# Expert stage of a four-block transformer kernel: four buffers for gathered rows and results, gathers six tiles ahead of the additions, addresses straight from the row table

## The chip, the cores and the metric

The kernel runs on one core of a Trainium2 chip. The metric is the device time of one execution in microseconds (us). Three runs of the kernel before took 780.53, 781.83 and 781.97 us, so the median is 781.83 us. Everything is computed in float32.

## The reference, cut to what matters

`x` has 16 sequences of 128 tokens with 256 features, 2048 rows in all. Four blocks are added to it one after the other, each on a normalised copy of the rows: a cross-attention, a slot block with 64 slots, a second cross-attention with 16 heads, and a mixture of 8 experts. The change touches only the last one:

```python
scores = softmax(x @ gate_w.T)                       # 2048 x 8
topk_ids, topk_w = grouped_topk(scores)              # best 2 of 4 groups, then best 2 experts; weights sum to 1
combine = zeros((T, 8)).at[arange(T)[:, None], topk_ids].add(topk_w)
gate, up = split(einsum('th,eih->tei', x, w13_weight))   # 256 -> 2 x 512 per expert
act = silu(gate) * up * combine[:, :, None]
out = einsum('tei,ehi->th', act, w2_weight)          # 512 -> 256, summed over the experts
```

A row has a weight other than zero for two experts only, so only those two are worth computing.

## The kernel before, in words

**Stages.** The first three blocks are software-pipelined over four groups of four sequences. They end at about 480 us of the span. The last normalised rows, each with its 8 expert weights behind it (`ROW` = 264 numbers), are stored in a table in device memory (`xh_d`), and the sum so far goes to `out_d`. A routing stage (up to about 503 us) sorts the 4096 pairs of row and expert by expert and cuts them into `NT` = 39 tiles of up to 128 rows, each tile for one expert. It leaves `row_no` (L189, one column of 128 row numbers per tile) and `e_id` (the expert of each tile). VectorE says that they are ready with `routed` (L1392).

**One tile of the expert stage** passes through these steps; t is the tile's number. All weights are in SBUF by then.

- `fetch(t)`, GpSimd, L364: an indirect DMA gathers the tile's 128 rows of `xh_d` into one of two buffers `XI`. Its addresses come from a column of their own, `row_in[u]`, and not from `row_no`.
- `pick(t)`, VectorE, L1396 to L1399: takes the weight of each row for this expert (`row_w`), and copies the row numbers of tile t+2 into `row_in[u]` (L1397).
- `turn_in(t)`, TensorE, 2 transposes into PSUM; `turned`, ScalarE, L586: copies them to `XIT`.
- `gate_up(t)`, TensorE, L948: 4 matmuls of 128x128 by 128x512, shown as 8 records. `gate(t)`, ScalarE, L590: Silu of the gate half. It waits for both halves (`gu_ps`). `gated(t)`, VectorE, L1404: Silu times weight times up.
- `turn_act(t)`, TensorE, 4 transposes; `turned(t)`, VectorE, L1408: copies them to `HAT`.
- `down(t)`, TensorE, L963: 4 matmuls of 128x128 by 128x256 (8 records). `answer(t)`, ScalarE, L595: copies the result to one of two buffers `YO`, which lie in `OT` (`y_ok`).
- `number(t)`, VectorE, L1412: copies the row numbers of tile t from `row_no` into `row_out[u]` (`no_ok`). It waits for `turns`, which GpSimd raises when it starts the addition before.
- `add(t)`, GpSimd, L374: an indirect DMA with addition adds the 128 results to rows of `out_d`. It waits for `y_ok`, for the landing of `add(t-1)` (`added`), and for `no_ok`.

Transposes on TensorE all have the line of a helper, L621.

**The order** on each engine is written by hand. Step t of TensorE is `turn_in(t+2)`, `gate_up(t+1)`, `down(t-1)`, `turn_act(t)`. Step t of ScalarE is `turned(t+2)`, `gate(t+1)`, `answer(t-1)`. Step t of VectorE is `pick(t+2)`, `gated(t+1)`, `turned(t)`, `number(t-1)`. These steps run in a loop of 18 turns with two steps each, with a few written out before and after it. GpSimd does `fetch(t+5)` right after `add(t)` (its constant `AHEAD` = 4 counts from the fetch that stands ahead of an addition), in a loop of 17 turns, two fetches and two additions a turn. `fetch(t)` waits until tile t-2 has been picked (L361) and transposed (L362), since it takes that tile's buffer.

```python
pool.wait_ge(picked_ok, t - 1)     # L361
pool.wait_ge(xt_ps, t - 1)         # L362
```

At the very end SyncE waits until all additions have landed (L293).

Of the kernel before, what the change touches and what calls it, by code (L numbers as in the profile page):

```python
# [7 lines left out]
ALU = mybir.AluOpType  # L8
# [3 lines left out]
P = 128  # L12
B, S, D = 16, 128, 256
# [13 lines left out]
NT = B * S * NPICK // P + NE - 1  # L27
EPS = 1e-5
# [32 lines left out]
def build(nc, x_d, ctx_d, ctxT_d, keep_d, fold_d, rows_d, experts_d, xh_d, out_d):  # L61
    with ExitStack() as stack:
# [67 lines left out]
        def split(v, t):  # L130
# [58 lines left out]
        row_no = sb("row_no", [P, NT + 2], mybir.dt.int32)  # L189
        row_w = [sb(f"row_w{u}", [P, 1]) for u in range(2)]  # L190
        row_w8 = [sb(f"row_w8{u}", [P, NE]) for u in range(2)]
        row_in, row_out = ([sb(f"{t}{u}", [P, 1], mybir.dt.int32) for u in range(2)] for t in ("row_in", "row_out"))
        at = KEEP["wih"][0]
        assert KEEP["aW2"][0] + KEEP["aW2"][1] - at >= 2 * (ROW + D + 2 * INTER)
        XI = [keep[:, at + ROW * n:at + ROW * (n + 1)] for n in range(2)]
        at += 2 * ROW
# [4 lines left out]
        YO = [spare_ot[:, D * n:D * n + D] for n in range(2)]  # L201
# [17 lines left out]
        weights_ok, weights_in, asked = sem("weights_ok"), sem("weights_in"), sem("asked")  # L219
        g_diff, g_exp, picks, counted, routed = (sem(t) for t in ("g_diff", "g_exp", "picks", "counted", "routed"))  # L220
        xi_in = [sem(f"xi_in{u}") for u in range(2)]
        xt_ps, xt, gu_ps, silu, act_ok, ha_ps, ha, y_ps, y_ok, picked_ok, no_ok, turns, added = (
            sem("e_" + t) for t in ("xt_ps", "xt", "gu_ps", "silu", "act_ok", "ha_ps", "ha", "y_ps", "y_ok", "picked_ok", "no_ok", "turns", "added"))
# [7 lines left out]
        AHEAD = 4  # L231
        XT_PS, Y_PS = ps[:, 4, 0:D], [ps[:, 5 + u, 0:D] for u in range(2)]

        def tiles_of(eng, step):
# [62 lines left out]
        def _(pool):  # L297
# [94 lines left out]
        def _(act):  # L392
# [186 lines left out]
            act.sem_inc(turns, 1)  # L579
            act.sem_inc(y_ok, 2)  # L580
# [3 lines left out]
            def turned(t, u):  # L584
                act.wait_ge(xt_ps, t + 1)
                act.copy(XIT[u], XT_PS.rearrange("p (k n) -> p k n", k=KD)).then_inc(xt, 1)  # L586

            def gate(t, u):
                act.wait_ge(gu_ps, t + 1)
                act.activation(HA[u], ps[:, 2 * u, :], ACT.Silu).then_inc(silu, 1)  # L590
# [6 lines left out]
            def step(t, u, half):  # L597
                turned(t + 2, u)
                gate(t + 1, 1 - u)
                answer(t - 1, 1 - u)  # L600

            turned(0, 0)
            turned(1, 1)
            gate(0, 0)
            turned(2, 0)
            gate(1, 1)
            tiles_of(act, step)
            gate(NT - 1, 0)
            for t in range(NT - 3, NT):
                answer(t, t % 2)  # L610
# [3 lines left out]
        def _(pe):  # L614
# [320 lines left out]
            def turn_in(t, u, half):  # L935
                pe.wait_ge(xi_in[u], 16 * (half + 1))
                if not isinstance(t, int) or t:
                    pe.wait_ge(xt, t)
                for k in range(KD):
                    ins = turn(XT_PS[:, k * P:(k + 1) * P], XI[u][:, k * P:(k + 1) * P])  # L940
                ins.then_inc(xt_ps, 1)

            def gate_up(t, u):
                at = pe.value_load(e_id[0:1, bass.ds(t, 1)], min_val=0, max_val=NE - 1) * EXP_N
                pe.wait_ge(xt, t + 1)
                for g in range(2):
                    for k in range(KD):
                        ins = pe.matmul(ps[:, 2 * u + g, :], XIT[u][:, k, :], experts[:, bass.ds(at + (2 * k + g) * INTER, INTER)],  # L948
                                        start=(k == 0), stop=(k == KD - 1))
                ins.then_inc(gu_ps, 1)  # L950

            def turn_act(t, u):
                pe.wait_ge(act_ok, t + 1)
                for k in range(INTER // P):
                    ins = turn(ps[:, 7, k * P:(k + 1) * P], HA[u][:, k * P:(k + 1) * P])
                ins.then_inc(ha_ps, 1)

            def down(t, u):
                at = pe.value_load(e_id[0:1, bass.ds(t, 1)], min_val=0, max_val=NE - 1) * EXP_N
                pe.wait_ge(y_ok, t + 1)  # L960
                pe.wait_ge(ha, t + 1)
                for k in range(INTER // P):
                    ins = pe.matmul(Y_PS[u], HAT[u][:, k, :], experts[:, bass.ds(at + 2 * KD * INTER + k * D, D)],  # L963
# [3 lines left out]
            def step(t, u, half):  # L967
                turn_in(t + 2, u, half + 1)
                gate_up(t + 1, 1 - u)
                down(t - 1, 1 - u)  # L970
                turn_act(t, u)

            turn_in(0, 0, 0)
            turn_in(1, 1, 0)
            gate_up(0, 0)
            turn_in(2, 0, 1)
            gate_up(1, 1)
            turn_act(0, 0)
            tiles_of(pe, step)
            gate_up(NT - 1, 0)  # L980
            down(NT - 3, 0)
            turn_act(NT - 2, 1)
            down(NT - 2, 1)
            turn_act(NT - 1, 0)
            down(NT - 1, 0)
# [3 lines left out]
        def _(dve):  # L989
# [390 lines left out]
            dve.memset(row_no[:, NT:NT + 2], 0)  # L1380
# [13 lines left out]
            def pick(t, u, half):  # L1394
# [117 lines left out]
```

## Time and profile before

| | |
|---|---|
| runs, median (lowest to highest) | 781.83 us (780.53 to 781.97) |
| profiled execution, span from first to last instruction | 779.1 us |
| TensorE matmuls, busy | 651.9 us, 84% of the span |
| VectorE, ScalarE, GpSimd, busy | 369.5, 221.6 and 181.0 us |
| expert stage, first gather issued to the end of the span | 504.0 to 779.1 us |
| moved by DMA | 40.27 MB, mean 52 GB/s |

The profile gives no time of its own for the profiled execution beside its span; the span is 2.7 us under the median of the runs. It lists each engine's instructions with start and duration, and for idle time what ended it. A line such as "PE ps L621 <- DMA keep<-normed,row_in" reads: TensorE, about to run line 621 with its output in `ps`, waited for the DMA from the row table (`normed`) into `keep` (where `XI` lies), addressed by `row_in`. "issue" is time in which nothing that the profile shows was waited for.

### The profile page before, as it was taken

To read this page: it belongs to the slowest core of one execution; us is meant where nothing else is said; L and a number is where in the kernel's file an instruction comes from. 1 tells how busy PE (TensorE), PEld (TensorE's weight loads), DVE (VectorE), ACT (ScalarE), POOL (GpSimd) and SP (SyncE) were. 2 spreads that over 40 slices of the span, in tenths; PEclk is the share of its full clock that TensorE was granted. 3 is DMA by queue.
4 is the path that set the end of the run, shared out by engine and by line. 5 is a ranking of instruction groups with operands and counts; after the bars stand their busy time and mean duration, and the time that the engine had idled before them with its cause. 6 is when DMAs were issued, how large, how long until landed. Compare 5 with 4: busy or idle time off the path is not lost.

```text
span 779.1 us, 10605 instructions
## 1 busy us (share of the span) xinstructions
PE 651.9 (84%) x3506; PEld 451.2 (58%) x3507; DVE 369.5 (47%) x925; ACT 221.6 (28%) x361; POOL 181.0 (23%) x151
## 2 busy tenths in 40 slices
PE   4968689998799988999978973198999989898993
PEld 3746457686477863768746752145555555555552
DVE  4443649638486384685536675622232222222221
ACT  1241254431455224454124410021221212121220
POOL 2100223002330013120022100413333333334332
PEclk9987799999999998999988995589999999999998
DMA  9900100002000011000070202012222222222222
GB/s 351 407 21 1 54 1 1 2 21 94 14 0 0 20 54 54 0 0 0 0 261 36 82 0 58 7 29 41 41 41 41 40 42 34 43 35 43 36 35 26
DMA packets 20756, 40.27 MB, mean 52 GB/s; under 512 B 3872, under 2 KB 17440, under 8 KB 19456
## 3 DMA queue, kind: packets, MB, share of 16 engines
q1 hardware_dynamic: 8736, 25.16, 8.6%
q0 software_dynamic: 7488, 10.39, 8.2%
q10 hardware_dynamic: 4512, 4.46, 1.7%
q8 instruction: 12, 0.20, 0.1%
q14 instruction: 8, 0.07, 0.0%
HBM read 30.37 MB, written 9.64 MB: 51 GB/s over the span
## 4 chain that ended last, share of the span: by engine, by line
PE 56%; issue 16%; DVE 8%; DMA 8%; ACT 5%; POOL 3%; DVEq 3%; POOLq 1%; ACTq 0%
PE ps L617 33%; PE ps L948 11%; PE ps L621 8%; DMA keep<-normed,row_in 6%; PE ps L963 4%; POOL var_xh L300 1%; ACT ring L482 1%; DVE mx L1127 1%; DMA out_x<-OT,row_out 1%; DVEq L1040 1%; ACT keep L586 1%; DVE ring L1131 1%; POOL ring L357 1%; DVE rc L1137 1%; DVE XH L1008 1%
## 5 line engine op out<-in xcount | busy, mean ns | idle before, releaser
L948 PE MATMUL ps<-experts,keep 128*128 x312 | 144.7, 607 | 8.1 <-ACT keep L586 7.8
L1404 DVE SCALAR_TENSOR_TENSOR keep<-keep,row_w,ps 128x512 f32<-128x512 f32 x39 | 29.2, 749 | 151.9 <-ACT keep L590 151.9
L948 PEld LDWEIGHTS ps<-experts,keep 128*128 128x128 f32 x312 | 56.9, 192 | 70.1 <-issue 69.7
L374 POOL DMA_INDIRECT out_x<-OT,row_out x39 | 61.8, 1584 | 147.9 <-DVE row_out L1412 86.6
L963 PE MATMUL ps<-experts,keep 128*128 x312 | 73.9, 380 | 2.0 <-DVE keep L1408 2.0
L300 POOL TENSOR_TENSOR var_xh<-var_xh,minus_half 128x4 f32<-128x4 f32 x16 | 16.9, 1059 | 250.4 <-DVE var_xh L1003 250.4
L617 PE MATMUL ps<-experts,keep 128*128 128x256 f32 (+1 forms) x184 | 70.1, 533 | 5.9 <-DVE experts L1067 2.8
L963 PEld LDWEIGHTS ps<-experts,keep 128*128 128x128 f32 x312 | 59.1, 190 | 26.2 <-issue 20.1
L617 PE MATMUL ps<-ring,V 128*32 128x128 f32 x512 | 64.3, 279 | 1.5 <-DVE OT L1139 1.5
L1127 DVE TENSOR_REDUCE mx<-ps 128x8 f32<-128x1024 f32 x32 | 39.1, 1220 | 53.8 <-PE ps L617 53.8
L617 PE MATMUL ps<-ring,keep 128*32 128x128 f32 x512 | 63.5, 273 | 0.0
L590 ACT ACTIVATE keep<-ps 128x512 f32<-128x512 f32 x39 | 23.4, 599 | 133.7 <-PE ps L948 133.7
L313 POOL TENSOR_TENSOR ring<-experts,keep 128x512 f32<-128x512 f32 x32 | 33.2, 1041 | 111.5 <-PE ps L617 111.5
L617 PEld LDWEIGHTS ps<-ring,keep 128*32 128x32 f32 x512 | 56.0, 110 | 0.0
L617 PEld LDWEIGHTS ps<-experts,keep 128*128 128x128 f32 x184 | 38.4, 215 | 27.7 <-issue 18.4
L621 PE MATMUL ps<-keep 128*128 128x128 f32 x234 | 36.6, 279 | 16.6 <-DMA keep<-normed,row_in 16.6
L488 ACT COPY ring<-ps 128x1024 f32<-128x1024 f32 x32 | 32.4, 1014 | 61.3 <-PE ps L621 60.9
L617 PEld LDWEIGHTS ps<-ring,V 128*32 128x32 f32 x512 | 45.7, 109 | 6.5 <-issue 6.4
L621 PEld LDWEIGHTS ps<-keep,ring 128*128 128x128 f32 x256 | 29.3, 146 | 26.9 <-ACT ring L482 22.7
L1137 DVE RECIPROCAL rc<-ps 128x128 f32<-128x128 f32 x32 | 30.6, 956 | 29.6 <-PE ps L617 29.6
L621 PE MATMUL ps<-keep,ring 128*128 128x128 f32 x256 | 36.4, 287 | 9.5 <-ACT ring L482 9.5
L364 POOL DMA_INDIRECT keep<-normed,row_in x39 | 38.7, 992 | 23.8 <-issue 11.0
(209 smaller groups left out, 942.9 us busy)
## 6 DMA issues: line engine op xcount, KB each, us to landing
experts<-in_experts SPq DMA_DIRECT2D x8, 1536.0 KB, 16.6
keep<-in_keep SPq DMA_DIRECT2D x1, 3075.0 KB, 19.1
ring<-in_fold SPq DMA_DIRECT2D x1, 2112.0 KB, 11.2
experts<-in_x SPq DMA_DIRECT2D x4, 512.0 KB, 3.5
experts<-in_ctxT SPq DMA_DIRECT2D x4, 512.0 KB, 4.1
out_x<-X ACTq DMA_DIRECT2D x4, 512.0 KB, 3.1
normed<-XH ACTq DMA_DIRECT2D x4, 512.0 KB, 4.0
experts<-in_ctx SPq DMA_DIRECT2D x4, 384.0 KB, 3.4
```

The costliest lines, as they stand in the source:

```text
L300: pool.tensor_tensor(var[name][:, :], var[name][:, :], minus_half[:, :], ALU.pow).then_inc(s["rs_" + name], 1)
L313: pool.tensor_tensor(KB[u % 2], KT[:, t, bb * S:(bb + 1) * S].unsqueeze(1).broadcast_to([P, HT4, S]), kept("head_mask").unsqueeze(2).broad ...
L364: pool.indirect_dma_start(out=XI[u], out_offset=None, in_=xh_d, in_offset=bass.IndirectOffsetOnAxis(ap=row_in[u][:, 0:1], axis=0)).then_in ...
L374: pool.indirect_dma_start(out=out_d, out_offset=bass.IndirectOffsetOnAxis(ap=row_out[u][:, 0:1], axis=0), in_=YO[u], in_offset=None, compu ...
L488: act.copy(PQ[u % 2], ps[:, 5:7, :].rearrange("p t (h n) -> p (t h) n", h=4)).then_inc(s["pt"], 1)
L617: ins = pe.matmul(out, w, m, start=(k == 0), stop=(k == len(pairs) - 1))
L621: return pe.transpose(out, t, ident)
L948: ins = pe.matmul(ps[:, 2 * u + g, :], XIT[u][:, k, :], experts[:, bass.ds(at + (2 * k + g) * INTER, INTER)], start=(k == 0), stop=(k == K ...
L963: ins = pe.matmul(Y_PS[u], HAT[u][:, k, :], experts[:, bass.ds(at + 2 * KD * INTER + k * D, D)], start=(k == 0), stop=(k == INTER // P - 1))
L1127: dve.tensor_reduce(mx[u % 2][:, :], sc, AXX, ALU.max)
L1137: dve.reciprocal(rc[u % 2][:, :], bank(o)[:, S:2 * S])
L1404: dve.scalar_tensor_tensor(HA[u], HA[u], row_w[u][:, 0:1], ps[:, 2 * u + 1, :], ALU.mult, ALU.mult).then_inc(act_ok, 1)
```

## The change

`XI`, `YO`, `row_w` and `row_w8` have four buffers (`DEEP` = 4) instead of two. `row_in` and `row_out` go, with the copies L1389, L1390, L1397 and L1412, the memset L1380 and the semaphores `asked`, `turns` and `no_ok`. Both indirect DMAs read their addresses from the tile's column of `row_no`. `fetch(t)` waits for tile t-4 instead of t-2, and `fetch(t+6)` comes right after `add(t)`. GpSimd's part has no loop any more, since its addresses are fixed columns. The loops of the other three engines have 8 turns of four steps, with five steps written out ahead. `gu_ps` becomes `g_ps` after the gate half and `u_ps` after the up half: Silu waits for the first alone, `gated` for both. The waits that protect buffers are written anew: `down(t)` waits for `answer(t-2)` and comes to that wait after the one for `ha`, and `answer(t)` waits until `add(t-4)` has landed. The order of the steps on TensorE, ScalarE and VectorE is as before.

```diff
+DEEP, AHEAD = 4, 6
-        row_no = sb("row_no", [P, NT + 2], mybir.dt.int32)
-        row_w = [sb(f"row_w{u}", [P, 1]) for u in range(2)]
-        row_in, row_out = ([sb(f"{t}{u}", [P, 1], mybir.dt.int32) for u in range(2)] for t in ("row_in", "row_out"))
+        row_no = sb("row_no", [P, NT], mybir.dt.int32)
+        row_w = [sb(f"row_w{u}", [P, 1]) for u in range(DEEP)]
...
-        YO = [spare_ot[:, D * n:D * n + D] for n in range(2)]
+        YO = [spare_ot[:, D * n:D * n + D] for n in range(DEEP)]
...
+        FIRST = DEEP + 1
         def tiles_of(eng, step):
-            with eng.Fori(0, (NT - 3) // 2) as m:
-                step(2 * m + 1, 1, m)
-                step(2 * m + 2, 0, m + 1)
+            for r in range(FIRST):
+                step(0, r)
+            with eng.Fori(0, (NT - 2 - FIRST) // DEEP) as m:
+                for r in range(FIRST, FIRST + DEEP):
+                    step(m, r)
...
-            def fetch(t, u):
-                if not isinstance(t, int) or t >= 2:
-                    pool.wait_ge(picked_ok, t - 1)
-                    pool.wait_ge(xt_ps, t - 1)
-                    pool.sem_inc(asked, 1)
-                pool.indirect_dma_start(out=XI[u], out_offset=None, in_=xh_d,
-                                        in_offset=bass.IndirectOffsetOnAxis(ap=row_in[u][:, 0:1], axis=0)).then_inc(xi_in[u], 16)
-            def add(t, u):
-                pool.wait_ge(y_ok, t + 3)
-                if not isinstance(t, int) or t:
-                    pool.wait_ge(added, 16 * t)
-                pool.wait_ge(no_ok, t + 1)
-                pool.sem_inc(turns, 1)
-                pool.indirect_dma_start(out=out_d, out_offset=bass.IndirectOffsetOnAxis(ap=row_out[u][:, 0:1], axis=0),
-                                        in_=YO[u], in_offset=None, compute_op=ALU.add).then_inc(added, 16)
+            def fetch(t):
+                if t >= DEEP:
+                    pool.wait_ge(xt_ps, t - DEEP + 1)
+                    pool.wait_ge(picked_ok, t - DEEP + 1)
+                pool.indirect_dma_start(out=XI[t % DEEP], out_offset=None, in_=xh_d,
+                                        in_offset=bass.IndirectOffsetOnAxis(ap=row_no[:, t:t + 1], axis=0)).then_inc(xi_in[t % DEEP], 16)
+            def add(t):
+                pool.wait_ge(y_ok, t + 1)
+                if t:
+                    pool.wait_ge(added, 16 * t)
+                pool.indirect_dma_start(out=out_d, out_offset=bass.IndirectOffsetOnAxis(ap=row_no[:, t:t + 1], axis=0),
+                                        in_=YO[t % DEEP], in_offset=None, compute_op=ALU.add).then_inc(added, 16)
...
-            for t in range(AHEAD + 1):
-                fetch(t, t % 2)
-            add(0, 0)
-            with pool.Fori(0, (NT - 1 - AHEAD) // 2) as m:
-                for t, u in ((2 * m + AHEAD + 1, 1), (2 * m + AHEAD + 2, 0)):
-                    fetch(t, u)
-                    add(t - AHEAD, u)
-            for t in range(NT - AHEAD, NT):
-                add(t, t % 2)
+            for t in range(AHEAD):
+                fetch(t)
+            for t in range(NT):
+                add(t)
+                if t + AHEAD < NT:
+                    fetch(t + AHEAD)
...
-            def answer(t, u):
-                act.wait_ge(y_ps, t + 1)
-                act.wait_ge(turns, t + 1)
-                act.copy(YO[u], Y_PS[u]).then_inc(y_ok, 1)
+            def answer(m, r):
+                act.wait_ge(y_ps, DEEP * m + r + 1)
+                if r >= DEEP:
+                    act.wait_ge(added, 16 * (DEEP * m + r - DEEP + 1))
+                act.copy(YO[r % DEEP], Y_PS[r % 2]).then_inc(y_ok, 1)
...
-                for g in range(2):
+                for g, done in enumerate((g_ps, u_ps)):
                     for k in range(KD):
                         ins = pe.matmul(...)
-                ins.then_inc(gu_ps, 1)
+                    ins.then_inc(done, 1)
...
-                pe.wait_ge(y_ok, t + 1)
                 pe.wait_ge(ha, t + 1)
+                if r >= 2:
+                    pe.wait_ge(y_ok, t - 1)
...
-            dve.tensor_copy(row_in[0][:, :], row_no[:, 0:1])
-            dve.tensor_copy(row_in[1][:, :], row_no[:, 1:2])
-            settle()
             dve.tensor_copy(mark[:, :], w_sum[:, 0:1]).then_inc(routed, 1)
...
-                dve.tensor_copy(row_in[u][:, :], row_no[:, bass.ds(t + 2, 1)])
...
-            def number(t, u):
-                dve.wait_ge(turns, t + 1)
-                dve.tensor_copy(row_out[u][:, :], row_no[:, bass.ds(t, 1)]).then_inc(no_ok, 1)
```

## Rows read from the trace of the kernel before

**Rows 1.** The page: busy us of each engine, share of the span, instructions.

```profile
PE 651.9 (84%) x3506; PEld 451.2 (58%) x3507; DVE 369.5 (47%) x925; ACT 221.6 (28%) x361; POOL 181.0 (23%) x151
```

**Rows 2.** Busy time by stretch: engines, granted clock, DMA share, GB/s.

```profile
200.00:300.00 100.00, 91.39 (x620) 68.28 (x620) 63.05 (x141) 41.12 (x60) 16.21 (x16) 1.00 0.07 25
...
560.00:580.00 20.00, 18.91 (x70) 11.46 (x69) 5.45 (x18) 4.04 (x9) 7.15 (x7) 1.00 0.24 40
```

**Rows 3.** Who waited for whom, 480 to 779 us: total us, times, longest.

```profile
PE ps L621 <- DMA keep<-normed,row_in: 16.6, 19, 5.5
...
PE ps L948 <- ACT keep L586: 7.8, 17, 0.5
```

**Rows 4.** Timeline of one pair of steps, 590 to 605 us: start, us, work.

```profile
590.67 0.82 PE L621 MATMUL ps<-keep 128*128 128x128 f32 x6
590.87 0.37 ACT L595 COPY OT<-ps 128x256 f32<-128x256 f32 x1 [1.13 <-PE ps L963]
...
591.91 0.14 DVE L1412 COPY row_out<-row_no 128x1 int32 x1
...
592.90 1.59 POOL L374 DMA_INDIRECT out_x<-OT,row_out  x1 [4.51 <-DVE row_out L1412]
...
594.79 0.99 POOL L364 DMA_INDIRECT keep<-normed,row_in  x1 [0.30 <-issue]
...
597.68 0.43 PE L621 MATMUL ps<-keep 128*128 128x128 f32 x2 [0.59 <-DMA keep<-normed,row_in]
...
598.55 3.69 PE L948 MATMUL ps<-experts,keep 128*128 x8 [0.44 <-ACT keep L586]
598.73 1.59 POOL L374 DMA_INDIRECT out_x<-OT,row_out  x1 [2.94 <-DVE row_w L1399]
...
600.62 0.99 POOL L364 DMA_INDIRECT keep<-normed,row_in  x1 [0.30 <-issue]
```

**Rows 5.** The chain that ended last, over one such pair.

```profile
594.79 2.76 DMA keep<-normed,row_in
597.55 0.13 issue
...
610.85 0.45 PE ps L621 x2
```

**Rows 6.** Timeline of the stage's start.

```profile
502.55 0.15 DVE L1389 COPY row_in<-row_no 128x1 int32<-128x1 int32 x1
...
502.84 0.15 DVE L1392 COPY mark<-ring 128x1 f32<-128x1 f32 x1
...
519.31 3.60 PE L948 MATMUL ps<-experts,keep 128*128 x8
...
525.12 3.60 PE L948 MATMUL ps<-experts,keep 128*128 x8
...
532.54 3.70 PE L948 MATMUL ps<-experts,keep 128*128 x8 [0.45 <-ACT keep L586]
```

**Rows 7.** Timeline of the stage's end.

```profile
749.84 3.60 PE L948 MATMUL ps<-experts,keep 128*128 x8
...
760.80 0.37 ACT L595 COPY OT<-ps 128x256 f32<-128x256 f32 x1 [1.13 <-PE ps L963]
...
761.99 1.55 POOL L374 DMA_INDIRECT out_x<-OT,row_out  x1 [3.11 <-DVE row_out L1412]
...
766.52 1.55 POOL L374 DMA_INDIRECT out_x<-OT,row_out  x1 [2.97 <-DVE row_out L1412]
...
770.91 1.55 POOL L374 DMA_INDIRECT out_x<-OT,row_out  x1 [2.84 <-DMA out_x<-OT,row_out]
```

**Rows 8.** DMA from 600 to 700 us: the only queue used, and issues to landing.

```profile
q0 software_dynamic: 2880, 4.00, 24.4%
...
out_x<-OT,row_out POOLq DMA_INDIRECT x16, 3.8
keep<-normed,row_in POOLq DMA_INDIRECT x15, 2.8
```

More of the change, by code:

```diff
@@ L578, in _, with turned, gate, step @@
             store(LAST)
-            act.sem_inc(turns, 1)
-            act.sem_inc(y_ok, 2)
             exp_gate(B - GB, B)
[L584 to L590, printed above, removed]
-            def answer(t, u):
-                act.wait_ge(y_ps, t + 1)
-                act.wait_ge(turns, t + 1)
-                act.copy(YO[u], Y_PS[u]).then_inc(y_ok, 1)
[L597 to L600, printed above, removed]
+            def turned(m, r):
+                act.wait_ge(xt_ps, DEEP * m + r + 1)
+                act.copy(XIT[r % 2], XT_PS.rearrange("p (k n) -> p k n", k=KD)).then_inc(xt, 1)
+            def gate(m, r):
+                act.wait_ge(g_ps, DEEP * m + r + 1)
+                act.activation(HA[r % 2], ps[:, 2 * (r % 2), :], ACT.Silu).then_inc(silu, 1)
+            def answer(m, r):
[3 more added lines that the diff above has]
+                act.copy(YO[r % DEEP], Y_PS[r % 2]).then_inc(y_ok, 1)
+            def step(m, r):
+                turned(m, r + 2)
+                gate(m, r + 1)
+                if r:
+                    answer(m, r - 1)
             turned(0, 0)
-            turned(1, 1)
+            turned(0, 1)
             gate(0, 0)
-            turned(2, 0)
-            gate(1, 1)
             tiles_of(act, step)
-            gate(NT - 1, 0)
+            gate(0, NT - 1)
             for t in range(NT - 3, NT):
-                answer(t, t % 2)
+                answer(0, t)
         @block.tensor
@@ L933, in _, with turn_in @@
             pe.wait_ge(routed, 1)
[L935 to L938, printed above, removed]
+            def turn_in(m, r):
+                pe.wait_ge(xi_in[r % DEEP], 16 * (m + r // DEEP + 1))
+                if r:
+                    pe.wait_ge(xt, DEEP * m + r)
                 for k in range(KD):
-                    ins = turn(XT_PS[:, k * P:(k + 1) * P], XI[u][:, k * P:(k + 1) * P])
+                    ins = turn(XT_PS[:, k * P:(k + 1) * P], XI[r % DEEP][:, k * P:(k + 1) * P])
@@ L964, in down, with step @@
                                     start=(k == 0), stop=(k == INTER // P - 1))
                 ins.then_inc(y_ps, 1)
[L967 to L974, printed above, removed]
+            def step(m, r):
+                turn_in(m, r + 2)
+                gate_up(m, r + 1)
+                if r:
+                    down(m, r - 1)
+                turn_act(m, r)
@@ L975, in _ @@
+            turn_in(0, 0)
+            turn_in(0, 1)
             gate_up(0, 0)
-            turn_in(2, 0, 1)
-            gate_up(1, 1)
-            turn_act(0, 0)
             tiles_of(pe, step)
[L980 to L985, printed above, removed]
+            gate_up(0, NT - 1)
+            down(0, NT - 3)
+            turn_act(0, NT - 2)
+            down(0, NT - 2)
@@ L988, in _ @@
+            turn_act(0, NT - 1)
+            down(0, NT - 1)
         @block.vector
@@ L1379, in _ @@
                               kept("expert_no").unsqueeze(1).broadcast_to([P, NT, NE]), ALU.is_equal)
-            dve.memset(row_no[:, NT:NT + 2], 0)
             dve.wait_ge(placed, 1)
@@ L1410, in number, with gated @@
-            def number(t, u):
-                dve.wait_ge(turns, t + 1)
-                dve.tensor_copy(row_out[u][:, :], row_no[:, bass.ds(t, 1)]).then_inc(no_ok, 1)
-            def step(t, u, half):
-                pick(t + 2, u, half + 1)
-                gated(t + 1, 1 - u)
-                turned(t, u)
-                number(t - 1, 1 - u)
-            pick(0, 0, 0)
-            pick(1, 1, 0)
+            def gated(m, r):
+                dve.wait_ge(silu, DEEP * m + r + 1)
+                dve.wait_ge(u_ps, DEEP * m + r + 1)
+                dve.wait_ge(picked_ok, DEEP * m + r + 1)
+                dve.scalar_tensor_tensor(HA[r % 2], HA[r % 2], row_w[r % DEEP][:, 0:1], ps[:, 2 * (r % 2) + 1, :], ALU.mult, ALU.mult).then_inc(act_ok, 1)
@@ L1422, in _, with turned, step @@
+            def turned(m, r):
+                dve.wait_ge(ha_ps, DEEP * m + r + 1)
+                dve.tensor_copy(HAT[r % 2], ps[:, 7, :].rearrange("p (k n) -> p k n", k=INTER // P)).then_inc(ha, 1)
+            def step(m, r):
+                pick(m, r + 2)
+                gated(m, r + 1)
+                turned(m, r)
+            pick(0, 0)
+            pick(0, 1)
             gated(0, 0)
-            pick(2, 0, 1)
-            gated(1, 1)
-            turned(0, 0)
             tiles_of(dve, step)
-            gated(NT - 1, 0)
@@ L1428, in _ @@
-            for t in range(NT - 3, NT):
-                if t > NT - 3:
-                    turned(t, t % 2)
-                number(t, t % 2)
+            gated(0, NT - 1)
+            turned(0, NT - 2)
+            turned(0, NT - 1)
 def packed(parts, width, arrays):
```

46 lines of the change are left out of this document (21 added, 25 removed).

## Prediction

> **What bounds the kernel now.** I read the page first, then the busy time by stretch, the list of waits, the chain of waits, and last the timeline of one pair of steps and of both ends of the stage. The page says that TensorE is the busy engine, 84% of the span [rows 1]. In the expert stage, busy time by stretch shows it at 18.9 of 20 us with the clock at its upper level, 2.4 GHz [rows 2]. That looks like an engine-bound stage, but a busy share of nine tenths hides a regular stall. The list of waits names it: 19 times TensorE waited for a gather before a transpose, and 17 times there was a second gap of 0.44 to 0.5 us before the matmuls behind it [rows 3].
>
> The chain of waits shows how regular: in every second step it leaves TensorE and goes through a gather that takes 2.76 us from issue to landing, and 0.13 us later TensorE starts. The chain is back at the same transposes at 610.85, after starting them at 597.68, so one pair of steps takes 13.17 us [rows 4, 5]. Near the end of the loop the pair takes 13.2 us as well; I counted 17 stalled steps, the first between 525.12 and 532.54.
>
> Two rows of the stage's start give the price of a step without the stall: 525.12 - 519.31 = 5.81 us. The next step has it: 532.54 - 525.12 = 7.42 us, 1.6 us more [rows 6]. So the second gap belongs to the stall. It is credited to ScalarE's copy of the tile just transposed, but `gate_up` needs the tile before that, and in steps without a stall it starts right after the two transposes. I read it as TensorE's sequencer, which had run ahead of the array and has lost that lead.
>
> Why every second step? In the timeline the result of tile t is copied out from 590.87 to 591.24. VectorE's `number` ends at 592.05, since it stands behind `turned` of the next tile, and `add(t)` starts at 592.90, 0.85 us later. The gather behind it is issued at 594.79, lands near 597.55, and is wanted when the four transposes before it end, at 597.09 (597.68 less the 0.59 us of waiting): 0.6 us too late, with the 0.13 us of waking. The stalled step is 1.5 us longer, and so the next gather, issued at 600.62 and landing about 603.4, is in time for the transposes at about 604.2 (598.55 and 5.82 less their own 0.2) [rows 4, 8]. GpSimd is not short of time: 1.59 + 0.30 + 0.99 = 2.9 us of instructions for each tile.
>
> **The change, part by part.**
>
> *Gathers one tile further ahead, in four buffers.* The gather behind `add(t)` is now for tile t+6 and is wanted one step of 5.82 us later. Its buffer was freed by tile t+2, which was transposed in step t, well before. *Addresses from the table.* The wait for `number` goes: `add(t)` can start about 0.8 us after the copy's end at 591.24 (by the 0.85 us from `number` to the addition; bounds 0.5 and 1.1), so at 592.1 and not 592.90. The gather then lands at 592.1 + 1.89 + 2.8 = 596.8, 5.7 us after its step's beginning at 591.12, and is wanted at 2 x 5.82 = 11.6 us: 5.9 us of slack where 0.6 was missing [rows 4, 8]. The new address costs the old reads: 128 numbers, one from each partition. That each number stands in a row of 39 and not alone in its tile changes nothing that I can price; the bounds are 0 and +0.5 us on each gather, which the slack hides either way. VectorE loses 2 x 0.15 us a tile, where it had room.
>
> *What is late next.* With no stall TensorE runs step after step at 5.82 us. Each other wait at that pace: `down` needs `turned` of a tile whose transposes ended 3.4 us before. Silu and `gated` have most of a step. `add` waits for the landing of the addition before: 3.8 us from issue, and 4.53 us from one addition to the next where that wait decides at the end (766.52 - 761.99), so 1.3 us of room in 5.82 [rows 7, 8]. `answer` waits for the addition four tiles before, which landed two steps earlier. So nothing takes the stall's place.
>
> *The loop itself.* 18 turns of two steps become 8 turns of four. The first step of a turn is just the one that stalls now, so a turn's own cost on TensorE (the branch, with the sequencer's lead spent) could lie hidden in the 1.57 us. From below it is 0: after the landing TensorE starts in 0.13 us, so the branch is done by then. From above it is the whole stall, 1.57 us, 8 times, 12.6 us. I take 0: between the turns the array has 0.45 + 1.7 us or more of queued work, and the start of the loop at 519.31 shows no gap at all. What it costs if that cover is gone is a rival below.
>
> *Silu after the gate half.* It starts 1.7 us earlier and nobody waits: 0 in the steady steps. At the very end `gated(38)` lies under `down(36)` and the transposes of tile 37 already, so 0 there; bounds -0.3 and 0. *Start.* Two copies and one drain go from before `routed`: 502.84 - 502.55 = 0.29 us [rows 6]. Gathers 2 and 3 now follow at once behind gather 1, and that one may land up to 0.3 us later: bounds 0 and -0.3, I take -0.3. The first tile's matmuls run at the lower clock level as before. *GpSimd without its loop*: 78 DMAs written out, with code to be loaded. Its slack of 5.9 us covers any gap that the stage shows now. *End.* The last three additions follow one another by their landings, at 761.99, 766.52 and 770.91 [rows 7]. Their waits keep one semaphore step fewer each: 0 to -0.3 us, I take -0.1.
>
> **Sum.** The step of `gate_up(2)` starts at 519.31 and that of `gate_up(37)` at 749.84, 35 steps later: 230.53 us. At 5.82 us they take 203.7 us, 26.8 less, which is also 17 stalls of 1.57 us [rows 6, 7]. With 0.3 at the start and 0.1 at the end it is 27.2 us. The span becomes 779.1 - 27.2 = 751.9 us. The median of the runs stands 2.7 us above the span, and I keep that: 781.83 - 27.2 = 754.6 us.
>
> **Rivals.**
>
> *A turn of the loop shows.* Four steps make a body twice as long. For it speaks that the stall and the turn fall together, so the trace has no turn without a stall. Against it: the 0.13 us, and that from 600 to 700 us, through seven turns, only the queue of the gathers and additions moved anything, so no code was loaded again [rows 8]. At half the upper bound, 0.8 us x 8 = 6.3 us, the time is 761; at the whole of it 767. The Trainium skill ("Runtime: NRT & Kernel Launch", Instruction fetch mechanics) says that a taken branch to code outside the two resident blocks must load it first, and that is the rule that speaks against a longer body; the rows agree that the shorter one is resident, and no row can say it of the longer. [...]
>
> *The stall stays.* It doesn't do what it says if the gather's lead is not what ends the wait, for example because gathers queue behind additions in the DMA and move late in any order. Then a step keeps its 6.6 us and the time is 781.5. Against it: each gather takes the same 2.8 us, issued 1.9 us behind an addition.
>
> *Slower: the additions become the bound.* Each waits for the one before to land. If closer spacing of the transfers, or one more gather in flight, stretches the landing from 3.8 us to beyond 5.8 (with the 0.75 us to wake GpSimd, more than 6.6 us per tile), the stage follows them. At 7.0 us of landing it is 7.75 us x 38 tiles, against 6.6 x 38 now, 44 us more: 826. Against it: the 16 DMA engines are busy 24% of the time [rows 8], an addition already follows another after 598.73 - 592.90 = 5.83 us in every second step [rows 4], and the landings don't stretch there.
>
> **How the numbers follow.** The forecast, 754.6, has a chance of 0.80; the turn of the loop shown by 2 us or more 0.12; the stall stays in full or nearly so 0.04; the additions bound it 0.04. The forecast's own uncertainty is about 2 us: half a microsecond in total of small edits, 0.02 us on a step of 5.82 times 37, and runs that spread by 1.4 us. The range reaches up into the loop's case, to 761, and down to 751.5, where a step would be 5.75 us. What this kernel's measurement can tell from no change is about 0.2%, 1.6 us. Faster by more than that: 0.80 + 0.12 and half of the stalled case, 0.94. Same: 0.02. Slower: 0.04.
>
> **What would show it.** In the profile after, the list of waits should have TensorE wait for gathers at the stage's start only (2 times or so, where there were 19), and no gap before `gate_up` behind it. Eight records of L948 should start every 5.82 us, and the chain of waits from 510 us on should be TensorE alone until the last additions. Gathers should land about 6 us before their transposes. A gap once every four steps, at the first transposes of a turn, would show the loop; additions that start 0.75 us after the landing of the one before, in the middle of the stage, would show the DMA bound. The prediction is wrong if a step is over 6 us without either, for then something that the stall covered costs time on TensorE itself.

## Result, and the profile after

| | before | after |
|---|---|---|
| runs | 781.87 us (780.53 to 781.97, 4 runs) | 753.5 us (744.58 to 756.64, 4 runs) |
| ratio | | 0.9603, 95% interval 0.955 to 0.9656 |
| the same comparison again, on another chip | 782.24 us (779.25 to 785.1, 17 runs) | 753.97 us (751.4 to 756.19, 5 runs) |
| ratio | | 0.9634, interval 0.9604 to 0.9664 |

The change makes the kernel faster. The first ratio, applied to the 781.83 us from which the forecast was made, is 750.8 us (746.6 to 754.9), the second 753.2 us (750.9 to 755.6). The forecast of 754.6 us lies inside both intervals, but the first ratio's centre lies 0.7 us below the range's lower end of 751.5. The run of 756.64 us, which is also the profiled one, counts as slow and is left out of the first ratio, so that this ratio rests on three runs. One of the three, 744.58 us, pulls it down: the mean of all four runs is 0.962 of the kernel before, which would be 752.3 us.

The page of the changed kernel, where [rows 1] showed TensorE at 84%, is from an execution with a span of 754.8 us:

```profile
PE 647.9 (86%) x3506; PEld 453.4 (60%) x3507; DVE 363.4 (48%) x844; ACT 221.8 (29%) x361; POOL 180.9 (24%) x151
```

Busy time by stretch (engines in the order of the page, then granted clock, DMA share, GB/s). Where [rows 2] had TensorE busy for 18.9 of 20 us, it has no gap left in 100:

```profile
600.00:700.00 100.00, 100.00 (x378) 62.46 (x377) 28.49 (x68) 23.48 (x52) 44.60 (x35) 1.00 0.28 46
```

Who waited for whom, 480 to 760 us, where [rows 3] had 19 waits for gathers. Two are left, both at the stage's start, and the gap before `gate_up` is gone with them:

```profile
PE ps L617 <- DMA keep<-normed,row_no: 5.7, 2, 5.1
...
PE ps L945 <- issue: 0.3, 1, 0.3
```

The chain of waits is TensorE alone, 5.82 us a step (545.95 - 540.13), for 35 steps. [Rows 5] had a gather in it at every second step.

```profile
540.13 3.44 PE ps L945 x8
543.57 1.73 PE ps L962 x8
545.29 0.66 PE ps L617 x6
545.95 3.44 PE ps L945 x8
```

A steady step, to be read against [rows 4]. The result's copy ends at 534.07, the addition starts at 534.35, and its gather is issued at 536.25:

```profile
533.70 0.37 ACT L592 COPY OT<-ps 128x256 f32<-128x256 f32 x1 [2.84 <-PE ps L962]
...
534.35 1.60 POOL L375 DMA_INDIRECT out_x<-OT,row_no  x1 [2.89 <-ACT OT L592]
...
536.25 0.99 POOL L367 DMA_INDIRECT keep<-normed,row_no  x1 [0.30 <-issue]
```

The stage's start and end, against [rows 6, 7]: the first gather, the third tile's matmuls, those of tile 37, and the last three additions.

```profile
506.70 1.19 POOL L367 DMA_INDIRECT keep<-normed,row_no  x1 [3.42 <-DVE mark L1385]
...
522.52 3.60 PE L945 MATMUL ps<-experts,keep 128*128 x8
...
726.13 3.60 PE L945 MATMUL ps<-experts,keep 128*128 x8
...
737.74 1.55 POOL L375 DMA_INDIRECT out_x<-OT,row_no  x1 [3.97 <-ACT OT L592]
...
742.19 1.55 POOL L375 DMA_INDIRECT out_x<-OT,row_no  x1 [2.90 <-DMA out_x<-OT,row_no]
...
746.61 1.55 POOL L375 DMA_INDIRECT out_x<-OT,row_no  x1 [2.87 <-DMA out_x<-OT,row_no]
```

From the first gather issued to the end of the span it is 754.8 - 506.7 = 248.1 us, and was 779.1 - 504.0 = 275.1 us: 27.0 us less. The 35 steps take 726.13 - 522.52 = 203.6 us, and took 230.5. But the first gather came 2.7 us later than before, in a part of the kernel that the change leaves as it was. So the time has two parts: the stage, where the sum came out within 0.2 us, and the blocks ahead of it, which move from execution to execution. The experiments take them in turn.

### The profile page after: what moved, and what is told of

It reads as the page before. It is cut to its first block, busy times and chain, and to the rows that moved or that the text cites. A ratio compares the mean times of both kernels' runs of the same rounds, so it can differ in the third digit from the quotient of the medians.

```text
span 754.8 us, 10099 instructions
## 1 busy us (share of the span) xinstructions
PE 647.9 (86%) x3506; PEld 453.4 (60%) x3507; DVE 363.4 (48%) x844; ACT 221.8 (29%) x361; POOL 180.9 (24%) x151
## 4 chain that ended last, share of the span: by engine, by line
PE 70%; issue 10%; DVE 8%; ACT 4%; POOL 2%; DVEq 2%; DMA 2%; POOLq 0%; ACTq 0%
PE ps L613 34%; PE ps L945 18%; PE ps L617 9%; PE ps L962 8%; POOL var_xh L304 1%; ACT ring L480 1%; DVE mx L1124 1%; DMA out_x<-OT,row_no 1%; DVEq L1037 1%; DVE ring L1128 1%; POOL ring L361 1%; DVE rc L1134 1%; DVE XH L1005 1%; DVE experts L1036 1%; ACT experts L404 1%
## 5 line engine op out<-in xcount | busy, mean ns | idle before, releaser
L375 POOL DMA_INDIRECT out_x<-OT,row_no x39 | 61.7, 1583 | 129.5 <-ACT OT L592 123.7
L613 PEld LDWEIGHTS ps<-experts,keep 128*128 128x128 f32 x184 | 38.0, 213 | 26.8 <-issue 18.7
L1402 DVE COPY keep<-ps 128x512 f32<-128x512 f32 x39 | 27.0, 693 | 52.8 <-PE ps L617 52.8
L592 ACT COPY OT<-ps 128x256 f32<-128x256 f32 x39 | 14.5, 373 | 113.6 <-PE ps L962 113.6
L617 PEld LDWEIGHTS ps<-keep,ring 128*128 128x128 f32 x256 | 28.6, 143 | 26.9 <-ACT ring L480 22.7
L367 POOL DMA_INDIRECT keep<-normed,row_no x39 | 38.6, 991 | 15.0 <-issue 11.3
```

Of the source, the lines that this page charges most:

```text
L367: pool.indirect_dma_start(out=XI[t % DEEP], out_offset=None, in_=xh_d, in_offset=bass.IndirectOffsetOnAxis(ap=row_no[:, t:t + 1], axis=0)) ...
L613: ins = pe.matmul(out, w, m, start=(k == 0), stop=(k == len(pairs) - 1))
L617: return pe.transpose(out, t, ident)
L1402: dve.tensor_copy(HAT[r % 2], ps[:, 7, :].rearrange("p (k n) -> p k n", k=INTER // P)).then_inc(ha, 1)
```

## Experiments on the stage

**The changed kernel again.** No edit.

> The changed kernel once more, unaltered, beside the kernel before. My theory: the expert stage is worth 27.1 us in every execution (17 stalls of 1.57 us and 0.3 us at the start), and what went beyond that in the first comparison came from the stages ahead of it, where TensorE's clock was granted at its lower level for 7 us at a time at up to four places, each worth 3 us, in some executions and not in others. Then from the first gather to the end the profile shows 248 us as in the first profile, whatever the whole time is, and whole times lie in steps of about 3 us between 742 and 757. Rival: the expert stage itself has a faster state (744.58 us was seen once), for example without the cold first tile; then a fast execution shows less than 246 us from the first gather to the end.

It gave 753.97 us, and its profile 754.4 - 506.1 = 248.3 us from the first gather to the end. That is the first profile's 248.1 within 0.2, though the whole times spread over 751.4 to 756.2. The kernel before spread over 779.25 to 785.1 in 17 runs of the same comparison, four times as wide as the 1.4 us that I had taken from three. None of the five was near 744.58, and the steps of 3 us that I expected between whole times can't be seen in them (751.4, 753.7, 754.0, 754.2 and 756.2). The rival, a faster state of the stage itself, can't be excluded for that one run; every profile of the changed kernel and of the versions with its lead and without extra matmuls ahead of the stage has 248.1 to 249.0 us.

**Straight addresses alone.** Gathers one tile less ahead.

```diff
-DEEP, AHEAD = 4, 6
+DEEP, AHEAD = 4, 5
```

> One size: AHEAD 5 instead of 6, so the gather behind the addition of tile t is for tile t+5, as in the kernel before; addresses stay straight from the row table. In the profile of the changed kernel an addition starts 0.41 us after the step's first transposes, its gather is issued 1.9 us later and lands 2.8 us after that, 5.1 us into a step of 5.82. So my theory expects 0.7 us of slack, no stall, and the time of the changed kernel within 1 us: the straight address alone removes the stall. Rival: the lead of one more tile is what removes it, and with five tiles every second step stalls again, 13.2 us a pair, about 780 us.

It gave 759.44 us, ratio 0.9722 (0.969 to 0.9753): neither the 754 of my theory nor the 780 of the rival. From the first gather to the end it is 252.8 us, so the straight address brings 22 of the stage's 27 us. The whole time is 5.5 us above the changed kernel's, and those need the sixth tile of lead. The list of waits gives no hint of them. It reads as in the changed kernel: one wait of 5.3 us for a gather, and no regular one. The distance between steps does:

```profile
604.91 3.63 PE L945 MATMUL ps<-experts,keep 128*128 x8
...
607.07 0.99 POOL L367 DMA_INDIRECT keep<-normed,row_no  x1 [0.30 <-issue]
...
610.10 0.82 PE L617 MATMUL ps<-keep 128*128 128x128 f32 x6
...
610.89 3.69 PE L945 MATMUL ps<-experts,keep 128*128 x8
```

The gather issued at 607.07 lands about 2.8 us later, at 609.9. Its transposes are the last two of the six that start at 610.10, so they are due at 610.54: 0.7 us of slack, as expected. Yet the step takes 610.89 - 604.91 = 5.98 us and not 5.82. In a full stall `gate_up` follows 0.87 us after the two transposes start (598.55 - 597.68 in [rows 4]), and without one after 0.2; here it follows 0.35 us after them (610.89 - 610.54). I read it so: a gather that lands 0.7 us ahead of its transposes leaves too little for those 0.87 us. That the sequencer does in them what comes between the two waits (reading `e_id`, the weights' addresses) is part of this reading; no run took it apart. Steps here are 5.91 and 5.88 to 6.17 us in turn, 5.95 on average, and 0.13 us x 35 = 4.6 us is most of the 5.5.

**Neither lead nor straight address.** The copy `number`, its tile and semaphores are back, the addition reads its addresses from that copy again, and AHEAD is 5.

```diff
+            def number(m, r):
+                if r:
+                    dve.wait_ge(turns, DEEP * m + r)
...
+                dve.tensor_copy(row_out[r % 2][:, :], src).then_inc(no_ok, 1)
...
+                pool.wait_ge(no_ok, t + 1)
+                pool.sem_inc(turns, 1)
```

> The changed kernel with two things as before: VectorE's copy of the row numbers for the addition (row_out, with its two semaphores), and AHEAD 5. Four buffers, loops of four steps and the early Silu stay. My theory: the addition starts about 0.85 us after VectorE's copy, so near 1.8 us into the step, the gather lands 6.5 us into a step of 5.82, and every second step stalls by 1.5 us again: 27 us slower than the changed kernel, within 2 us of the kernel before. Rival: the two buffers were what held the gathers back, and with four of them the time stays at that of the changed kernel.

It gave 784.87 us, ratio 1.0036 (1.0017 to 1.0054). The stalls are back, 19 waits for gathers as in [rows 3], with four buffers in place. So the number of buffers by itself does nothing, and the rival falls. The gathers' own addresses stayed straight here; no run put the copy `row_in` back.

```profile
605.03 3.69 PE L949 MATMUL ps<-experts,keep 128*128 x8
...
611.41 0.43 PE L621 MATMUL ps<-keep 128*128 128x128 f32 x2 [0.52 <-DMA keep<-normed,row_no]
```

**Lead alone.** The same with AHEAD 6.

> The changed kernel with VectorE's copy of the row numbers for the addition as before, and the gathers six tiles ahead kept. So the lead alone, without the straight address of the addition. With five tiles of lead the straight address alone still cost 5.5 us over the changed kernel, since a gather that lands only 0.7 to 0.9 us before its transposes leaves TensorE's sequencer no lead. My theory: six tiles of lead and a gather issued 0.9 to 1.3 us later still leave over 4 us, so no step stalls: the time of the changed kernel within 1.5 us. Rival: the copies and the extra semaphores cost by themselves (the version with five tiles and the copies was 2.7 us slower than the kernel before), and the time is 757 us or more.

It gave 755.91 us, ratio 0.9618 (0.9585 to 0.9651), the changed kernel's within the interval, and every steady step of its profile is 5.81 or 5.82 us. The copy and its semaphores cost nothing in the steps once the gathers have lead. From the first gather to the end it is 249.0 us, 0.8 more than in the changed kernel, all of it in the last additions. By the ratios, since the third was run on another chip, the four combinations are 1.0036 (neither), 0.9722 (address), 0.9618 (lead) and 0.9634 (both): the lead alone does all of it within the intervals, the address alone most of it, and they don't add up.

**Less lead than before.** AHEAD 4.

> One size: AHEAD 4. The gather for tile t+4 then follows the addition of tile t and is wanted at the first transposes of the very step in which that addition starts. My theory of a latency loop: from a step's start 5.95 us to the result's copy, 0.28 to the addition, 1.9 to the gather's issue, 2.8 to its landing and 0.13 to the transposes, so 11.1 us a step, some 36 steps at 5.2 us more, 185 to 195 us slower than the changed kernel: about 940 us. Rival (the stall is a fixed cost of a wait, not of the lead): one stall of 1.6 us in each step, about 810 us.

It gave 1026.7 us. The direction and the mechanism are those of my theory: TensorE waited 37 times for a gather, 186.2 us in all. But I expected 11.1 us a step, and it is 13.7:

```profile
619.12 1.59 POOL L375 DMA_INDIRECT out_x<-OT,row_no  x1 [10.77 <-ACT OT L592]
621.01 0.99 POOL L367 DMA_INDIRECT keep<-normed,row_no  x1 [0.30 <-issue]
623.94 0.68 PE L617 MATMUL ps<-keep 128*128 128x128 f32 x2 [5.14 <-DMA keep<-normed,row_no]
624.85 5.46 PE L945 MATMUL ps<-experts,keep 128*128 x8 [0.23 <-issue]
...
632.79 1.59 POOL L375 DMA_INDIRECT out_x<-OT,row_no  x1 [10.79 <-ACT OT L592]
```

The eight records of `gate_up` take 5.46 us and not 3.60, since the clock falls to its lower level in every step. Over 100 us it is granted at 0.76 on average:

```profile
600.00:700.00 100.00, 62.21 (x168) 33.25 (x167) 13.14 (x29) 10.02 (x22) 18.05 (x14) 0.76 0.11 19
```

So a wait of 5.1 us a step costs 7.9 us: the wait, 1.9 us of `gate_up` at the lower clock (5.46 - 3.60), and 0.7 us between the transposes and `gate_up` (624.85 - 623.94 = 0.91 where it is 0.2), which my 11.1 had left out as well. The 1.5 us stalls of the kernel before never did that ([rows 2] have 1.00).

**Silu after both halves**, as before the change.

```diff
-                act.wait_ge(g_ps, DEEP * m + r + 1)
+                act.wait_ge(u_ps, DEEP * m + r + 1)
```

> The changed kernel, but Silu waits for the up half as before. My theory: nobody waits for Silu in any step, and at the end the last VectorE product lies under other work, so 0 us, within 0.5. Rival: the early Silu is what let the whole stage run without a gap and its loss costs 0.6 us or more a step, 20 us.

It gave 755.74 us, ratio 0.9627 (0.9598 to 0.9655), steps of 5.82 us and 248.3 us from the first gather to the end: 0, as forecast.

## Experiments ahead of the stage

The granted clock by stretch, first of the changed kernel and then of the version with extra matmuls in the earlier loop, which is told below. In [rows 2] the clock of the stretch from 200 to 300 us was 1.00; the changed kernel's execution has a fall near 200 us that the one of before did not have:

```profile
198.00:210.00 12.00, 8.91 (x23) 3.91 (x21) 4.47 (x7) 5.82 (x8) 3.83 (x3) 0.72 0.00 0
...
395.00:425.00 30.00, 22.92 (x118) 14.28 (x117) 13.46 (x20) 10.82 (x13) 7.19 (x7) 0.83 0.49 188
```

```profile
198.00:210.00 12.00, 10.27 (x47) 6.65 (x46) 4.83 (x6) 4.86 (x6) 2.41 (x2) 1.00 0.00 0
395.00:425.00 30.00, 25.66 (x179) 16.99 (x177) 15.10 (x15) 13.84 (x16) 5.16 (x5) 0.89 0.34 124
```

**Extra matmuls in the earlier loop**, 128x128 by 128x256, whose result nobody reads, in TensorE's waits of 0.7 and 0.9 us:

```diff
+                busy(1, 0, 256)
                 turn_x4(n)
+                busy(2, 0, 256)
                 turn_x3(n + 1)
```

> The changed kernel with three extra matmuls of 128x128 by 128x256 in each turn of the loop of the earlier blocks, into TensorE's waits before the transposes of the last and of the next rows; nobody reads the result. The clock falls to its lower level for 7 us some 12 us behind that place in each of three turns and once more after the loop, and each fall costs 3 us. My theory: it is the thinner work there that lets it fall, and the run of 744.58 us was one without three of the four falls; with the extra work up to three falls go, 3 to 9 us faster. Rival: three short matmuls are too little or in the wrong place, the falls stay, and the time is that of the changed kernel within 1.5 us.

It gave 749.91 us, ratio 0.9568 (0.954 to 0.9597), 5 us less than the changed kernel by the ratios (0.9568 to 0.9634). Its six runs lie in two groups: 748.56 to 748.93 with a mean clock of 0.939 to 0.941, and 750.89 to 753.29 with 0.928 to 0.933. In the profiled one the first gather came at 498.8, 7.3 us earlier than in the changed kernel's second profile, with the fall near 200 us gone and less of them after 395 us, as the two rows above show. Not all of that belongs to the extra matmuls, as the table at the end of this section shows.

**The same edit in the kernel before.**

> The kernel before, unchanged in its expert stage, with the three extra matmuls in each turn of the earlier loop. My theory: the falls of the clock belong to the earlier blocks, which the change does not touch, so they go here as well, 3 to 7 us faster than the kernel before, and the expert stage still takes 275 us. Rival: the falls came more often in the changed kernel because of it, and the kernel before gains less than 1 us.

It gave 777.47 us, ratio 0.9935 (0.9907 to 0.9963), so 5.1 us faster, as much as in the changed kernel. From the first gather to the end it still took 777.1 - 501.9 = 275.2 us. The gain is no matter of the change. But my theory had the falls go, and in this profile three are left, between 200 and 210, 305 and 310, and 410 and 415 us.

**Extra matmuls ahead of the stage**, seventeen of 128x128 by 128x512 in TensorE's waits from the last gate logits on:

```diff
+            busy(3, 6, 512)
             pe.wait_ge(picks, 2)
...
+            busy(5, 6, 512)
+            pe.wait_ge(tiles_hot, 1)
+            busy(3, 6, 512)
...
+                if k == B:
+                    busy(2, 6, 512)
...
+            busy(4, 6, 512)
             pe.wait_ge(routed, 1)
```

> The changed kernel with 17 extra matmuls of 128x128 by 128x512 whose result nobody reads, in TensorE's waits between the last gate logits and the first transposes of the expert stage. In the profile TensorE runs at its lower clock level there for 48 us, to the end of the first tile's matmuls, which take 6.4 us and not 3.4. My theory: the level is held down by TensorE's idle time, so with work in the waits the first tile's matmuls take 3.4 to 3.6 us and some transposes and the placing matmuls are shorter too: 3 to 4 us faster. Rival: the clock stays at its lower level through the extra work, which then takes twice its time and delays the stage: 1 to 4 us slower.

It gave 752.26 us, ratio 0.9587 (0.9563 to 0.9611), 3.5 us less than the 755.7 and 755.9 us of the versions without such matmuls in the same comparison; the intervals of the ratios overlap a little. From the first gather to the end it is 246.6 us, 1.6 less than 248.2. The first tile's matmuls take 4.88 us where they took 6.40, and not the 3.4 to 3.6 that I expected; the clock had risen and fell once more at their start (0.50 from 508 to 510 us, 1.00 from 498 to 506). The placing matmuls take 0.75 us for 16 and not 1.20.

```profile
500.80 0.75 PE L934 MATMUL ps<-ring 128*128 128x78 bf16 x16
...
508.88 4.88 PE L956 MATMUL ps<-experts,keep 128*128 x8 [0.28 <-issue]
```

**Both sets.**

> The changed kernel with both sets of extra matmuls: three in each turn of the earlier loop (which alone gave 749.9 us, where the changed kernel in the same comparison's unit would be near 756) and seventeen ahead of the expert stage (alone 752.3 us). My theory: they act on separate stretches of low clock and add up, 6 us and 3.5 us: about 746 us. Rival: they overlap, since the falls are counted from the same start and move when the stage ahead is shorter, and the time stays near 750.

It gave 750.58 us, ratio 0.96 (0.9563 to 0.9636), from 748.56 to 755.58: by the medians they don't add up, and my 746 was wrong. The profiled run, 748.56 us, still had the falls near 197 and 303 us.

**Two more pairs in the loop**, before the transposes of the context and before the queries, where TensorE waits 1.35 and 1.25 us:

```diff
+                busy(2, 2, 256)
                 turn_context(n + 1)
+                busy(2, 1, 256)
                 query(n + 1)
```

> As the version with both sets, and two more pairs of extra matmuls of 128x128 by 128x256 in each turn of the earlier loop, before the transposes of the context and before the queries, where TensorE waits 1.35 and 1.25 us. In the version with the loop's three, two falls of 7 us were left, near 301 and 407 us, just at this place. My theory: they go too, in most executions, and the time is 3 to 6 us less than with both sets, about 742 us. Rival: they delay the chain by what they take beyond the waits, 0.4 us or more a turn, and the falls stay: 1 to 3 us slower than with both sets.

It gave 746.53 us (744.7 to 750.14), ratio 0.9534 (0.9499 to 0.957), 4.1 us less than with both sets, as expected, if not the 742. This is the fastest version, faster than both kernels: 4.7% less than the kernel before, and 1.0% less than the changed one by the ratios (0.9534 to 0.9634). In its profile the clock stays up in two of the places where it used to fall, and nearly so in the third:

```profile
190.00:220.00 30.00, 26.95 (x139) 17.67 (x139) 17.72 (x40) 13.34 (x23) 10.25 (x10) 1.00 0.19 63
300.00:315.00 15.00, 13.27 (x63) 7.91 (x62) 8.70 (x14) 8.00 (x11) 6.43 (x5) 1.00 0.10 34
395.00:425.00 30.00, 24.83 (x182) 16.75 (x181) 16.24 (x18) 13.79 (x16) 6.14 (x6) 0.94 0.43 163
```

**The parts of each profile.** In each of the loop's three turns ScalarE takes up the queries at one place of its own, and that row can be found in every profile. In the version with two more pairs:

```profile
107.24 1.45 ACT L404 ACTIVATE experts<-ps,q_col,keep 128x512 f32<-128x512 f32 x2 [1.49 <-PE ps L613]
208.95 1.45 ACT L404 ACTIVATE experts<-ps,q_col,keep 128x512 f32<-128x512 f32 x2 [1.49 <-PE ps L613]
310.67 1.45 ACT L404 ACTIVATE experts<-ps,q_col,keep 128x512 f32<-128x512 f32 x2 [1.49 <-PE ps L613]
```

With the first gather these rows cut the span into five parts (us):

| profile | to turn 1 | turn 1 to 2 | turn 2 to 3 | turn 3 to first gather | to the end |
|---|---|---|---|---|---|
| before | 103.0 | 101.7 | 104.7 | 194.5 | 275.1 |
| changed | 104.0 | 104.4 | 104.8 | 193.5 | 248.1 |
| changed, again | 103.5 | 104.4 | 104.8 | 193.5 | 248.3 |
| AHEAD 4 | 101.8 | 101.7 | 104.7 | 194.1 | 521.7 |
| changed, extra in the loop | 101.6 | 101.7 | 104.7 | 190.8 | 248.3 |
| before, extra in the loop | 104.1 | 104.4 | 103.1 | 190.4 | 275.2 |
| changed, extra ahead of the stage | 101.3 | 104.4 | 104.8 | 193.1 | 246.6 |
| changed, both sets | 101.1 | 104.4 | 104.8 | 189.7 | 246.8 |
| changed, both and two more pairs | 107.2 | 101.7 | 101.7 | 190.3 | 247.1 |

The loop's three matmuls take 3 us off the fourth part in every profile that has them, in both kernels: 189.7 to 190.8 us, where the nine profiles without them have 193.1 to 195.1. The missing fall near 200 us is not shown to be their work, since two of the nine lack it too (101.7). Both turns at 101.7 us stand only in the last version, in one profile. By their parts the two sets do add up: 3.8 us less in the fourth part and 1.5 less in the fifth than in the changed kernel's second profile. The medians don't show it, because the first part, which comes before most of the extra matmuls, varies by 6 us, 101.1 to 107.2 over all profiles, and by 5.5 us (101.1 to 106.6) over those that have no extra matmuls in it. There too the clock falls in one execution and not in the other. The same eight matmuls with both sets, and with two more pairs:

```profile
17.80 3.68 PE L613 MATMUL ps<-experts,qk 128*128 128x512 f32 x8
```

```profile
18.89 6.63 PE L613 MATMUL ps<-experts,qk 128*128 128x512 f32 x8
```

Against the changed kernel the extra matmuls and the clock that they hold up are worth 7.4 us by the medians (753.97 - 746.53, on two chips), and no list of waits shows them.

## Why the prediction was right, and where it was not

*The steps.* Right: 5.82 us each, 203.7 us forecast for 35 and 203.6 measured. The stalls were 26.8 us and are gone. The whole change was to gain 27.2 us. The stage gained 27.0 from its first gather on, and 27.3 with the 0.3 us ahead of that gather.

*The cause of the stall.* Right, and narrower than I put it. The two edits that I named, the lead and the straight address, are each nearly enough. For the second I had the addition start 0.8 us after the result's copy; it starts 0.28 us after it (534.35 - 534.07), and the 0.85 us after `number` belonged to the longer chain of semaphores. With the true figure the slack is 6.5 us and not 5.9, of no effect here.

*The loop's turns.* I took 0 of a possible 12.6 us. All steps are 5.81 or 5.82 us, turns included, so 0 was right. By the Trainium skill ("Runtime: NRT & Kernel Launch", Instruction fetch mechanics) a body beyond the two resident blocks would be loaded again at each turn; the body of four steps shows no gap at its turns, and from 600 to 700 us of the changed kernel, again, no queue but that of the gathers and additions moved anything.

*What is late next.* Nothing, as forecast. The additions' landings stay at 3.8 us and the gathers' at 2.8 with closer spacing.

*Start and end.* The two copies' 0.3 us at the start came: VectorE's last instruction before the first gather follows the row table by 0.27 us and no longer by 0.56. But from the first gather to the third tile's matmuls it is now 522.52 - 506.70 = 15.8 us, and was 15.3, since the first tile's matmuls ran at the lower clock for longer (6.40 us against 5.77). At the end I had 0.1 us, and it is 0.6: from the matmuls of tile 37 to the third last addition 737.74 - 726.13 = 11.6 us, where it was 12.1, again the addition that starts sooner after the copy. The last additions are 4.45 and 4.42 us apart, where they were 4.53 and 4.39 [rows 7].

*The step that failed* is the last one, the range, with its term "runs that spread by 1.4 us", and under it the part of the sum ahead of the stage, which was carried over as it stood ("the median of the runs stands 2.7 us above the span, and I keep that"). The whole time fell by 31.0 us in the first comparison (781.83 - 750.8) and by 28.6 in the second, of which the change explains 27.3; the other 3.7 and 1.3 us lie ahead of the stage or in the draw of the runs. The 1.4 us came from three runs on one chip that lay close together. In 17 runs on another chip the kernel before spreads over 5.9 us, and the changed one over 12 in nine runs on two chips. The 0.2% that I took to be what the measurement can tell was 0.5% for the first ratio and 0.3% for the second.

I had looked at the clock in the expert stage only. Between 190 and 425 us it falls to 1.2 GHz for 3 to 7 us at up to four places. One turn of the loop took 104.4 us with such a fall and 101.7 without, 2.7 to 3.1 us a fall. The first 104 us differ by up to 6 us, with more time at the lower clock in the longer ones (mean 0.82 in the longest, 0.87 to 0.89 in the shortest). In the 17 runs the four shortest, 779.3 to 780.3 us, have a mean clock of 0.937 to 0.939, and the three longest, 784.7 to 785.1, have 0.926 to 0.928. So the spread goes with the clock, and it is there without the change.

What the run of 744.58 us was stays open. Its mean clock of 0.946 over 742.6 us means some 24 us less at the lower level than 0.931 over 751.5. That is as much as three falls of 7 us, or one or two and a short first part. It was not profiled and did not come again. That it fell among the three runs of the ratio is luck, and so is that the forecast of 754.6 lies only 1.4 us from the second result: the spread could have moved it by as much.

One small slip stands in the range itself: its lower end of 751.5 us means steps of 5.73 us (3.1 us over 35 steps), not 5.75.

## What to carry to other kernels

A latency loop that missed its slot by half a microsecond cost 1.5 us in every second step here, and either a little more lead or a little less latency removed nearly all of it; price both, since they don't add up. A gather that landed 0.7 us before it was needed was still too late by 0.13 us a step, and such a shortage stands in no list of waits, only in the distance between steps. About 1 us of slack is my estimate of what is enough, from the 0.87 us; no run lies between 0.7 us and over 4. Before giving a range, look at the granted clock of the whole kernel, the stages that aren't touched included, and not at the spread of three runs. To compare versions in such a kernel, cut each profile into parts at rows that all of them have, since the whole times here hide 3 us of gain behind 6 us of spread in a part that the edits leave nearly alone.

## What the runs showed of the hardware

A wait of 5.1 us in steps of 13.7 us lets TensorE's clock fall to 1.2 GHz in each step, while waits of 0.6 us in pairs of 13.2 us don't. The same matmuls took 5.46 and 3.60 us. In stretches where TensorE works with waits of 0.5 to 1.4 us between thin pieces, the clock falls in some executions and not in others near 200 us (2.7 us each time), and in all but the version with the most extra matmuls near 305 us. Matmuls whose result nobody reads, put into such waits, made both kernels 5 us faster by the ratios and brought 1% in the best version.
